# Four layers on one core: the last head rows of layer 0, its output product and row norm, a weight product of layer 2 and the transposed norm of layer 1 in one block

## What is computed

```
out = out @ Wo + bo
x = out + hidden_state
mu, var = mean(x), var(x)            # over the 512 of a row
x = (x - mu) * rsqrt(var + 1e-6) * gamma + beta
```

```
xa = _ln(x, ln1_w, ln1_b)            # eps 1e-5
sx = concat([state, xa[:, :-1]]) - xa
xxx = xa + sx * maa_x
```

## Time and profile before

| | us |
|---|---|
| median of 3 runs (2637.67 to 2645.3) | 2638.56 |
| the profiled execution's own time | 2634.76 |
| its span in the trace | 2633.0 |
| PE / DVE / ACT / POOL busy | 2451.7 / 1384.9 / 1132.2 / 874.8 |

### The profile page before, as it was taken

How to read it: one execution, slowest core, us unless ns; L and a number is a source line. 1 busy time by engine, 2 the same in 40 slices (tenths; PEclk the granted TensorE clock), 3 DMA queues, 4 the chain that set the end, 5 groups by cost and what they waited for, 6 DMA issues and landing times. The chain is left out here.

```text
span 2633.0 us, 37868 instructions
## 1 busy us (share of the span) xinstructions
PE 2451.7 (93%) x13976; PEld 2161.6 (82%) x13976; DVE 1384.9 (53%) x2328; ACT 1132.2 (43%) x2441; POOL 874.8 (33%) x514
## 2 busy tenths in 40 slices
PE   7898689989998689899999999989999999999698
PEld 5676334479896457799999999989998999999698
DVE  4566641288886632333366665633335566564642
ACT  4687121232323332222466666622236666664320
POOL 1100322252220450442264553516217364451300
PEclk9999889999999799999999999999999999999799
DMA  7553163599994257434665555534266566653300
GB/s 236 129 137 71 67 232 114 152 240 237 239 238 156 68 180 241 146 141 151 219 218 196 185 187 169 183 110 171 108 227 213 182 199 193 208 182 94 130 2 25
DMA packets 196347, 432.94 MB, mean 164 GB/s; under 512 B 57820, under 2 KB 92660, under 8 KB 195396
## 3 DMA queue, kind: packets, MB, share of 16 engines
q1 hardware_dynamic: 196164, 430.52, 53.0%
HBM read 332.35 MB, written 106.27 MB: 167 GB/s over the span
## 5 line engine op out<-in xcount | busy, mean ns | idle before, releaser
L2104 PE MATMUL att_ring<-ca_pp,att_arena 128*128 128x400 f32 (+1 forms) x2304 | 433.5, 346 | 9.7 <-issue 7.8
L2104 PEld LDWEIGHTS att_ring<-ca_pp,att_arena 128*128 128x128 f32 (+1 forms) x2304 | 419.5, 189 | 16.0 <-issue 15.7
L2205 POOL TENSOR_TENSOR att_arena<-att_arena 128x1448 fp32r<-128x1448 f32 x64 | 211.7, 3308 | 474.7 <-ACT att_arena L2212 319.1
L2104 PE MATMUL att_ring<-att_arena,qk_wh 128*128 128x362 f32 x1024 | 257.1, 333 | 0.0
L2836 DVE TENSOR_TENSOR ca_yl<-att_ring,att_arena 128x400 fp32r<-128x400 f32 x256 | 146.4, 572 | 193.7 <-ACT att_arena L2797 193.7
L2104 PEld LDWEIGHTS att_ring<-att_arena,qk_wh 128*128 128x128 f32 x1024 | 186.3, 193 | 0.0
L2104 PE MATMUL att_ring<-att_arena,qk_wl 128*128 128x362 f32 x512 | 173.6, 339 | 9.9 <-POOL att_arena L2392 9.2
L2797 ACT ACTIVATE att_arena<-att_ring 128x400 fp32r<-128x400 f32 x256 | 128.8, 503 | 86.4 <-PE att_ring L2104 86.1
L2218 ACT ACTIVATE l_kstage<-att_score,att_shift 100x362 f32<-100x362 f32 x256 | 143.6, 562 | 44.5 <-DVE att_shift L2231 44.5
L1188 ACT ACTIVATE rec_stage<-rec_fbank,rec_columns 128x361 f32<-128x361 f32 x128 | 71.8, 563 | 193.9 <-PE rec_fbank L2104 193.2
L2104 PE MATMUL att_score<-att_arena 128*100 128x362 f32 x768 | 143.1, 336 | 1.5 <-POOL att_arena L2190 1.5
(11 more groups left out here) (408 smaller groups left out, 5954.3 us busy)
## 6 DMA issues: line engine op xcount, KB each, us to landing
att_arena<-ctx_parts SPq DMA_DIRECT2D x64, 1024.0 KB, 5.8
att_arena<-keys SPq DMA_DIRECT2D x64, 724.0 KB, 4.6
att_arena<-ctx_parts SPq DMA_DIRECT2D x64, 420.0 KB, 6.9
keys<-rec_stage SPq DMA_DIRECT2D x32, 724.0 KB, 4.3
keys<-l_kstage SPq DMA_DIRECT2D x32, 724.0 KB, 3.2
l_arena<-kept_value SPq DMA_DIRECT2D x176, 100.0 KB, 5.9
queries<-att_loose SPq DMA_DIRECT2D x64, 200.0 KB, 4.7
att_arena<-queries SPq DMA_DIRECT2D x64, 200.0 KB, 3.0
```

Source lines behind the costliest of these rows:

```text
L2104: issued = nc.tensor.matmul(out, x, y, start=(first and k == 0), stop=(last and k == count - 1))
L2205: self.nc.gpsimd.tensor_tensor(self.kl[:, n % 2].bitcast(F32R), self.kl[:, n % 2], self.kh[:, n % 2].bitcast(F32), ALU.subtract).then_inc( ...
```

## The change

The last batch's quad 1 is no longer normalised in the attention block: `HeadRows.normalise(dve, 1)` and both quads' stores are run in a new block. That block, `output_and_two_norms`, replaces the output product, both blocks of the row norm, the weight product beside them and both blocks of the transposed norm. Each engine goes in rounds n: DVE normalises batch n-2 for the transposed norm, adds the product to batch n and takes its statistics, and moves batch n-1 through gamma and beta and takes its second statistics. The statistics' small steps (aggregate, negated mean, variance plus eps, reciprocal) are done per batch and not for all eight together. Centring moves from DVE to ACT, and ACT applies all four chunks of the transposed norm. PE has two banks for the output product, two for the weight product, two for the turned rows; the weight product's four parts stand in rounds 3, 5, 7 and 8. SP loads w_k and w_q first, stores the head rows, loads layer 1's small tiles and layer 2's other two weights, stores the weight product and waits until that has landed. The four 1 MB weights of layer 1 are issued behind the block, since their room is free only then. One semaphore clearing stands behind the new block; the one between the layers is gone.

```diff
+class HeadRows:
+
+    def __init__(self, nc, sc):
+        self.nc = nc
+        self.outT = sc.sb("outT", [P, B, CC, L])
...
+    def normalise(self, dve, quad):
+        b, nc = B - 1, self.nc
+        dve.wait_ge(self.av_done, QUADS * b + quad + 1)
+        nc.vector.stream_shuffle(self.sums[:], self.mixed[:, 0:HG * L], [D0] * 32).then_inc(self.sums_done, 1)
+        dve.wait_ge(self.sums_done, quad + 1)
+        nc.vector.reciprocal(self.share[:], self.sums[:]).then_inc(self.share_done, 1)
+        dve.wait_ge(self.share_done, quad + 1)
+        dve.wait_ge(self.y_out[quad], 80 * b)
+        nc.vector.tensor_tensor(self.y[:, quad, :], self.mixed[:, 0:HG * L], self.share[:], ALU.mult).then_inc(self.y_done, 1)
+
+    def store(self, sp, b, quad):
+        sp.wait_ge(self.y_done, QUADS * b + quad + 1)
+        for j in range(4):
+            row = (4 * quad + j) * D0
+            sp.dma_start(self.outT[row:row + D0, b].rearrange("d h l -> d (h l)"),
+                         self.y[32 * j:32 * j + D0, quad, :]).then_inc(self.y_out[quad], 16)
+
...
                     widen_inverse(b - 1)
-            store_output(B - 1, 0)
-            store_output(B - 1, 1)
             sp.wait_ge(late_in, 16 * len(late))
...
                 if n < total and b and i == 2:
-                    finish(b - 1, 0)
+                    keep_mixed(b - 1, 0)
                 if n < total and b and i == AV_LATE + 3 * PIECES + 2:
-                    finish(b - 1, 1)
+                    keep_mixed(b - 1, 1)
-            for quad in range(QUADS):
-                normalise(B - 1, quad)
+            rows_out.normalise(dve, 0)
...
-def layer_norm_rows(nc, prefix, X, eps, gamma, beta, ready, next_stats, operands, parts, stored):
...
+def output_and_two_norms(nc, prefix, end, X, ident, ahead, room, gate, cur, query_weight_from, key_weight_from, parts, stored,
+                         norm_scale, norm_offset, eps_rows, eps_turned, loads):
+
+    RING_Z = 3
+    PRODUCT_AT = (3, 5, 7, 8)
+    flat = "p b c l -> p (b c l)"
+    with Scope(nc, prefix) as sc:
+        outT, Wo = end.rows.outT, end.Wo
+        oh, ol = ahead.fwh, ahead.fwl[:].bitcast(F32R)
...
+        @block.sync
+        def _(sp):
+            sp.dma_start(key_weight, key_weight_from).then_inc(weights_in, 16)
+            sp.dma_start(query_weight, query_weight_from).then_inc(weights_in, 16)
+            for quad in range(QUADS):
+                end.rows.store(sp, B - 1, quad)
+            loads(sp)
+            for n in range(CC):
+                sp.wait_ge(product_high, n + 1)
+                sp.dma_start(parts[:, 0, n, :], end.high[:, n, :].bitcast(F32)).then_inc(stored, 16)
+                sp.wait_ge(product_low, n + 1)
+                sp.dma_start(parts[:, 1, n, :], end.low[:, n, :].bitcast(F32)).then_inc(stored, 16)
+            sp.wait_ge(stored, 32 * CC)
+
+        @block.tensor
+        def _(pe):
+            def first_output(bank):
+                pe.wait_ge(z_high, 1)
+                for c in range(CC):
+                    pe.wait_ge(out_high, c + 1)
+                    nc.tensor.matmul(bank, zh[:, 0, c, :], oh[:, c, :], start=(c == 0), stop=False)
+                pe.wait_ge(z_low, 1)
+                for c in range(CC):
+                    nc.tensor.matmul(bank, zl[:, 0, c, :], oh[:, c, :], start=False, stop=False)
+                for c in range(CC):
+                    pe.wait_ge(out_low, c + 1)
+                    last = nc.tensor.matmul(bank, zh[:, 0, c, :], ol[:, c, :], start=False, stop=(c == CC - 1))
+                last.then_inc(z_full, 1)
+
+            def output(b):
+                pe.wait_ge(z_low, b + 1)
+                if b >= 2:
+                    pe.wait_ge(added, b - 1)
+                products(nc, zbank[b % 2][0:L, :], [((zh[:, b % RING_Z, c, :], zl[:, b % RING_Z, c, :]), (oh[:, c, :], ol[:, c, :]))
+                                                    for c in range(CC)]).then_inc(z_full, 1)
+
+            def weight_product(n):
+                if n == 0:
+                    pe.wait_ge(weights_in, 32)
+                if n >= 2:
+                    pe.wait_ge(product_low, n - 1)
+                for c in range(CC):
+                    last = nc.tensor.matmul(pbank[n % 2][:], query_weight[:, c, n * P:(n + 1) * P], key_weight[:, c, :],
+                                            start=(c == 0), stop=(c == CC - 1))
+                last.then_inc(product_full, 1)
+
...
+            for n in range(B + 2):
+                if n == 0:
+                    first_output(zbank[0][0:L, :])
+                elif n < B:
+                    output(n)
+                if n in PRODUCT_AT:
+                    weight_product(PRODUCT_AT.index(n))
+                if n >= 2:
+                    turn(n - 2)
+
+        @block.scalar
+        def _(act):
+            def high_source(b):
+                if b >= RING_Z:
+                    act.wait_ge(z_full, b - RING_Z + 1)
+                if b == B - 1:
+                    end.rows.last_arrived(act)
+                nc.scalar.activation(zh[:, b % RING_Z], outT[:, b], ACT.Copy).then_inc(z_high, 1)
+
+            def centre(b):
+                act.wait_ge(away_done, b + 1)
+                if b >= 2:
+                    act.wait_ge(scaled_done, b - 1)
+                nc.scalar.activation(centred[:, b % 2, :], X[:, b, :], ACT.Identity, bias=away[:, b:b + 1]).then_inc(centred_done, 1)
+
+            def root(k, b, ready, done):
+                act.wait_ge(ready, b + 1)
+                nc.scalar.activation(std[:, k, b:b + 1], vareps[:, k, b:b + 1], ACT.Sqrt).then_inc(done, 1)
+
+            def affine(b):
+                act.wait_ge(turned_ready, b + 1)
+                for c in range(CC):
+                    nc.scalar.activation(cur[:, b, c, :], turned[b % 2][:, c, 0:L], ACT.Identity, bias=norm_offset[:, c:c + 1],
+                                         scale=norm_scale[:, c:c + 1]).then_inc(affine_done, 1)
+
+            def keep_high(n):
+                act.wait_ge(product_full, n + 1)
+                nc.scalar.activation(end.high[:, n, :], pbank[n % 2][:], ACT.Copy).then_inc(product_high, 1)
+
+            high_source(0)
+            for c in range(CC):
+                nc.scalar.activation(oh[:, c, :], Wo[:, c, :], ACT.Copy).then_inc(out_high, 1)
+            high_source(1)
+            for n in range(B + 3):
+                if 0 <= n - 3 < B:
+                    affine(n - 3)
+                if n + 2 < B:
+                    high_source(n + 2)
+                if n < B:
+                    centre(n)
+                    root(0, n, var_ready, std_ready)
+                if 0 <= n - 1 < B:
+                    root(1, n - 1, again_var, again_std)
+                if n in PRODUCT_AT:
+                    keep_high(PRODUCT_AT.index(n))
+
+        @block.gpsimd
+        def _(pool):
+            def low_source(b):
+                pool.wait_ge(z_high, b + 1)
+                nc.gpsimd.tensor_tensor(zl[:, b % RING_Z], outT[:, b], zh[:, b % RING_Z].bitcast(F32), ALU.subtract).then_inc(z_low, 1)
+
+            for b in range(2):
+                low_source(b)
+            for n in range(B):
+                if n + 2 < B:
+                    low_source(n + 2)
+                pool.wait_ge(centred_done, n + 1)
+                if n >= 2:
+                    pool.wait_ge(moved, n - 1)
+                nc.gpsimd.tensor_tensor(scaled[:, n % 2, :], centred[:, n % 2, :], end.gamma[:], ALU.mult).then_inc(scaled_done, 1)
+
+        @block.vector
+        def _(dve):
+            def add(b):
+                dve.wait_ge(z_full, b + 1)
+                nc.vector.tensor_tensor(X[:, b, :], X[:, b, :], zbank[b % 2][0:L, :], ALU.add).then_inc(added, 1)
+                dve.wait_ge(added, b + 1)
+                nc.vector.bn_stats(stats[:, 0, b, :], X[:, b, :]).then_inc(summed, 1)
+                dve.wait_ge(summed, b + 1)
+                nc.vector.bn_aggr(moments[:, 0, b, :], stats[:, 0, b, :]).then_inc(moments_done, 1)
+                dve.wait_ge(moments_done, b + 1)
+                nc.vector.tensor_scalar(away[:, b:b + 1], moments[:, 0, b, 0:1], -1.0, None, ALU.mult).then_inc(away_done, 1)
+                nc.vector.tensor_scalar(vareps[:, 0, b:b + 1], moments[:, 0, b, 1:2], eps_rows, None, ALU.add).then_inc(var_ready, 1)
+
+            def move(b):
+                dve.wait_ge(std_ready, b + 1)
+                nc.vector.reciprocal(rstd[:, 0, b:b + 1], std[:, 0, b:b + 1]).then_inc(rstd_ready, 1)
+                dve.wait_ge(rstd_ready, b + 1)
+                dve.wait_ge(scaled_done, b + 1)
+                nc.vector.scalar_tensor_tensor(X[:, b, :], scaled[:, b % 2, :], rstd[:, 0, b:b + 1], end.beta[:],
+                                               ALU.mult, ALU.add).then_inc(moved, 1)
+                dve.wait_ge(moved, b + 1)
+                nc.vector.bn_stats(stats[:, 1, b, :], X[:, b, :]).then_inc(again_summed, 1)
+                dve.wait_ge(again_summed, b + 1)
```

(61 more changed lines are left out.)

172 lines of the change are left out of this document (72 added, 100 removed).

## The result

| | before | after |
|---|---|---|
| median of the runs, us | 2638.56 | 2616.33 (2614.81 to 2620.8) |
| span of the profiled execution, us | 2633.0 | 2614.4 |
| end of PE's last head row, us | 264.79 | 266.35 |
| VectorE's first difference, us | 341.60 | 321.81 |
| the seam between the two, us | 76.81 | 55.46 |

The changed kernel takes 0.9915 of the time of before (95% interval 0.9898 to 0.9931), 22.2 us less by the medians. Forecast were 15.7 less, 2622.9, with a range of 2615 to 2633. The result lies 1.3 above the lower end of the range, between the forecast and the shorter path of rival 3 (2615.2). The spans differ by 18.6: the seam is 21.35 shorter, the last head row ended 1.56 later (over all traces of this case it ends between 262.6 and 268.2, so that is no effect of the change), and the part behind the seam took 1.2 more.

The account below looks back on a forecast made before the run. PE bounds the whole program, but DVE paces the new block: entry, DVE's 46.2 us and exit start the difference at 325.85, not 341.60. 2634.8 less 15.7 is 2619.1, against the median 2622.9; range 2615 to 2633.

Parts of the forecast that it names:

- rival 3: New block: full clock from the second batch, no hold-up, small steps at half: 23.4 less, 2615.2; with the forecast 0.74.
- Entry: Start of the new block: exit 0.67, PE starts at 266.6, second batch's product in at 275.5.
- DVE's stretch: From 275.5 DVE sets the pace: adds, moves, normalisings, low parts, quad 1 and waits sum to 46.2, ending at 321.7.
- Root waits: DVE's normalising after a move waits for ACT's root: 0.3 in each of five rounds, 1.5.
- Small steps: Seven small DVE instructions per batch at 0.17 to 0.20 each; the skill's table would give 0.06, sum 5 to 6 shorter.
- Hold-ups by POOL: DVE shifts in the new block delayed by POOL: 1.05 each, one and a half of them counted, 1.5.
- rival 1: DVE's shift waits for POOL's multiplication by gamma in every batch: +6.8, 2629.7; chance 0.16.
- Exit: Block's end: last low part at 321.7, landing 2.3 plus issue to 324.5, exit with clearing 1.35, difference at 325.85.
- What hides: PE's 37 of DVE's 46 us, ACT, POOL and SP's loads and stores run beside DVE and cost nothing.
- Rival 2: PE's clock stays at 1.2 GHz through the block, PE leads: end at 343.7, 2640.7, slower than before; chance 0.10.
- Layer 1's loads: Issued behind the block, beside the difference: cost nothing; if one did wait, a few us, bounded by the 4.92 issue.

Follow-up runs that it names:

- e5: The changed kernel unaltered, run again: median 2619.47 us, 0.9926 of the kernel before; seam 55.82 us.
- e9: The changed kernel unaltered, a third time: median 2618.73 us, 0.9918 of the kernel before; seam 56.21 us.
- e10: The changed kernel with epsilon as the bias of ACT's root instead of DVE's one-column additions: 2618.95 us, 0.9921 of the kernel before; seam 54.55 us.
- e12: The changed kernel with POOL's remainder of the rounded source behind its gamma multiplication from batch 3 on: 2617.73 us, 0.9909 of the kernel before.
- e6: The changed kernel with the weight product's four parts one round earlier (2, 4, 6, 7): 2620.51 us, 0.9929 of the kernel before; seam 57.57 us.
- e7: The changed kernel with weight products one round earlier, epsilon in ACT's root and quad 1 normalised in round 0: 2616.40 us, 0.9910 of the kernel before.
- e2: The changed kernel with four more PE matmuls before each output product of batches 1 to 7: 2622.47 us, 0.9929 of the kernel before; seam 57.33 us.
- e11: The changed kernel with epsilon in ACT's root and quad 1 normalised in round 0: 2622.00 us, 0.9930 of the kernel before; seam 55.73 us.
- e3: The changed kernel with quad 1 normalised at the end of the attention block again: 2624.05 us, 0.9935 of the kernel before; seam 56.94 us.
- e8: The kernel before with only layer 1's four last loads issued behind the block's exit: 2641.39 us, 1.0005 of the kernel before; seam 72.43 us.
- e1: The changed kernel with one more DVE statistics operation per batch: 2620.47 us, 0.9922 of the kernel before; seam 58.71 us.
- e4: The new block with its work in stages (all adds, all moves, all normalisings): 2632.43 us, 0.9968 of the kernel before; seam 67.08 us.

## Why the prediction was right, and where its sizes were off

The mechanism held in the main, direction and range with it: one entry and one exit, DVE setting the pace between them, PE hidden beside it. Two parts of it did not hold, the place of POOL's hold-ups and the worth of layer 1's loads at the old exit. The forecast seam was 61.06, and 55.46 came: 5.6 us, in the terms of the sum:

- **Entry.** The second batch was in 8.96 after the rows, forecast 10.71. PE started 0.3 sooner, mostly because the block's exit took 0.32, not 0.67. The rest, 1.4, is the clock. I had taken 275.5 between a start at full and at half clock, by pauses like that of the earlier trace rows; the first twelve matmuls took 4.5 instead of 4.9, and the second twelve ran at full clock, as rival 3 had it. Some of this is luck: in e5 and e9, the same kernel, the second add came 0.75 later.
- **DVE's stretch.** 42.61 instead of 46.2. Adding took 1.80 (1.9), moving 2.00 (2.05), normalising 0.66 (0.85), a low part 0.60 (0.69), quad 1's normalising 3.8 (3.9). The mis-sized term is the normalising: the row of 0.54 is a duration, and the next instruction starts 0.46 behind its start. Over the 8 that is 0.9, and 0.6 more is the little I had added for POOL, which did not come. Low parts and adds were priced too high in the same way, by 1.1 together. Root waits: four of 0.27, not five of 0.3.
- **Small steps.** They last 0.14 to 0.18 each, a little less than the rows had it. Their cost on the path is the distance between starts, 0.07 or 0.2; e10, which takes 15 of them out, measures 0.12 each. The estimate of 0.06 each was worked out from the table of the page VectorE: DVE Perf Modes of the Trainium skill (section on the TRN2 errata). As a duration it is too low by these rows; as a cost it had the direction right, but not 5 to 6 us.
- **Hold-ups by POOL, rival 1.** 1.17 in two shifts, forecast 1.5. The size is near, but the place was wrong: not the multiplication by gamma, but POOL's subtraction ahead of it; e12 and the rows of the two shifts show this. I also counted the six undisturbed shifts of the earlier trace rows against the rival, where DVE had only started first. The page SBUF — State Buffer ("Who interferes with whom") of the Trainium skill says of two such operations that they exclude each other and whoever starts first goes on; the traces agree in both orders, and the hold-up is what is left of POOL's operation, less 0.2. It did not come in every batch, because POOL was idle when six of the eight shifts started.
- **Exit.** 3.90, forecast 4.15. Where ACT ended last (e6, e7), exit and clearing took 1.64, not 1.35; SP's issue and landing have the other 2.3.
- **What hides.** PE was busy for 33 of the 41.8 us from 280 to the difference and DVE never waited for it behind the second add; the loads and stores held up nobody. Both right. That PE's slack was "just covered" is what e2, e6, e11 and e12 show: a little more on PE, or a longer pause, and DVE waits 1.0 to 1.8 in one or two rounds.
- **Rival 2, the clock.** In the changed kernel PE was at half clock once after the entry, for most of 281 to 285 (0.57) behind a pause of 2.9, and DVE did not notice; from 285 to the end of DVE's stretch the clock was 1.00. So the rival did not come. Nor did a pause of this length always do it: after 2.49 and 2.86 (e5, e3) the clock stayed at 1.00.
- **Layer 1's loads.** I costed their new place at nothing and their old one as part of the 15.7. In e8 they were worth nothing by themselves, for the larger part since PE's product waited for a load beside them. In the changed kernel that product starts at 321.89 and waits for no load. It is only with layer 2's two weights issued early that the exit's gain is real; this is read from the rows, and no run has the new block with these loads late. I had not seen this second wait: in the earlier trace rows I read SP and DVE, and not what PE waited for at the same place.

What stays open is why PE's clock rises and falls at other points in executions of one kernel, and where the 1.1 us of e3's seam come from; no run tested either.

## What to carry to other kernels

When stages with different limits follow each other, doing them batch by batch in one block saves twice: in one block with the stages kept, 9.7 us went here, and the time in which each stage waits for its own slow engine was another 11.6. Count an engine's chain by the distance between starts, not by durations. Once two engines are nearly balanced, an edit that relieves one must not make the other pause: after a pause of 4.84 us PE came back at half clock, and the relief was gone. And before a rule is made of one trace, look at a second trace of the same kernel: the first twelve matmuls of this block took 4.5 us in one and 5.2 in another.

Before moving a wait out of a path, look for a second one that ends at the same time: the loads behind the exit shortened the seam by 4.4 us and the kernel by nothing that could be measured.

## What the runs showed of the hardware

- A DVE shift (two SBUF inputs) that starts in a GpSimd operation of two SBUF inputs, ahead of its last 0.2 us, ends 0.55 after it: 0.75 becomes 1.04 to 1.67, in 17 of 17 cases. One with a single large SBUF input (0.55 alone) that starts in the same GpSimd operation ended 0.28 after it and took 0.63 to 0.89 (four cases, e12).
- The same GpSimd multiplication takes 1.26 to 1.30 alone. Where it starts in a DVE shift that is held up it took 1.49 to 1.72, and 1.64 or 1.65 where it started 0.15 behind a shift of the kernel before, so both lose.
- A one-column DVE step lasts 0.14 to 0.18 and costs 0.07 from start to start when nothing is waited for, about 0.2 to one that reads its result.
- With the same pause of 1.52 or 1.53 us before them, PE's first twelve matmuls of the block took between 4.05 and 5.44 us in eleven traces (4.48, 4.79 and 5.20 in three of one kernel), and 5.43 after a pause of 5.46.
- After pauses of 3.45, 4.61 and 4.84 us (e1, e6, e11) PE's clock was 0.50 from its first matmul on, for 5.4 to 6.2 us. After pauses of 2.5 to 2.9 us within the block it stayed at 1.00 in three traces (e3, e5, e10) and was down to 0.50 within 1.3 us of work in four (the changed kernel's first, e4, e9, e12).
